# Edge counting in windows of 16 nodes instead of 32, and small operations shifted across five phase borders

## The reference

```python
xn = _layernorm(x)
x = x + gnn(xn, edge_index) + mix(xn[None])[0]
x = x + ffn(_layernorm(x)[None])[0]
```

```python
q, k, v = split(x @ qkv_w.T + qkv_b)                 # 8 heads of 96
phi_q = exp(einsum(q, rf) - q_norm); phi_k = exp(einsum(k, rf) - k_norm)
kv = einsum('bhnm,bhnd->bhmd', phi_k, v)
attn = einsum('bhnm,bhmd->bhnd', phi_q, kv) / maximum(denominator, 1e-6)
out = attn @ proj_w.T + proj_b
```

## Time and profile before

| | us |
|---|---|
| median of 3 runs | 2090.27 (2078.87 to 2092.76) |
| the profiled execution's own time | 2086.34 |
| its span | 2084.6 |
| PE busy in the span | 1991.5 (96%) |
| DVE busy in the span | 1168.3 (56%) |

### The profile page before, as it was taken

The page is one execution under the profiler, slowest core; times in us unless marked ns, Lnnn a source line. Parts: engine busy times, 40 slices in busy tenths (PEclk is TensorE's granted clock), DMA queues, the critical chain, the costliest instruction groups (busy, mean ns, idle before and its releaser), DMA issues. The chain is left out here.

```text
span 2084.6 us, 32353 instructions
## 1 busy us (share of the span) xinstructions
PE 1991.5 (96%) x9933; PEld 1469.9 (71%) x9934; DVE 1168.3 (56%) x2548; ACT 449.5 (22%) x822; POOL 176.6 (8%) x181
## 2 busy tenths in 40 slices
PE   4999899998989998999999999999997999999998
PEld 3666666666648887888888855556655777777776
DVE  6666436652565664888888652167764333333343
ACT  3222222222002321222222200004321222222222
POOL 0000000000000000000000000000001333222232
PEclk9999999998999999999999999999997999999999
DMA  7000220002645350743333244444225888899654
GB/s 257 22 17 20 93 107 17 20 17 74 217 120 171 121 155 32 221 146 102 122 101 112 82 153 156 151 134 142 90 74 196 271 249 241 252 284 289 180 136 83
DMA packets 81192, 282.79 MB, mean 136 GB/s; under 512 B 11689, under 2 KB 32225, under 8 KB 71490
## 3 DMA queue, kind: packets, MB, share of 16 engines
q1 hardware_dynamic: 59138, 211.02, 30.4%
q0 software_dynamic: 14848, 56.18, 11.1%
q10 hardware_dynamic: 7104, 14.26, 2.0%
HBM read 217.43 MB, written 63.99 MB: 135 GB/s over the span
## 5 line engine op out<-in xcount | busy, mean ns | idle before, releaser
L1379 PE MATMUL gat_Z<-h_head,first_rest 125*125 125x256 f32 (+1 forms) x1600 | 355.5, 381 | 3.3 <-DVEq L1283 3.3
L1379 PEld LDWEIGHTS gat_Z<-h_head,first_rest 125*125 125x125 f32 x1600 | 298.4, 189 | 49.2 <-issue 4.0
L762 PE MATMUL mix_G<-mix_w,xnT 128*125 128x384 f32 x720 | 243.0, 488 | 0.0
L762 PEld LDWEIGHTS mix_G<-mix_w,xnT 128*125 128x125 f32 x720 | 133.3, 189 | 85.1 <-issue 2.7
L2400 DVE TENSOR_SCALAR ex_idS<-ex_ids 128x1 int32 x52 | 8.0, 153 | 204.5 <-DMA out_rows<-ex_y,ex_idS 204.5
L2487 PE MATMUL ex_PH<-ex_xT,w_and_experts 128*128 128x128 f32 x936 | 111.1, 278 | 1.7 <-issue 0.2
L2487 PE MATMUL ex_PH<-ex_xT,ex_w 128*128 128x128 f32 x936 | 111.0, 278 | 0.8
L2487 PEld LDWEIGHTS ex_PH<-ex_xT,w_and_experts 128*128 128x128 f32 x936 | 106.5, 192 | 2.7 <-issue 2.7
L2497 PE MATMUL ex_PY<-w_and_experts,ex_hT 128*128 128x384 f32 x312 | 107.5, 495 | 0.3 <-ACT ex_hT L2434 0.3
L2497 PE MATMUL ex_PY<-ex_w,ex_hT 128*128 128x384 f32 x312 | 107.4, 494 | 0.3 <-ACT ex_hT L2434 0.3
L2487 PEld LDWEIGHTS ex_PH<-ex_xT,ex_w 128*128 128x128 f32 x936 | 106.5, 192 | 1.5 <-issue 1.3
(11 more groups left out here) (399 smaller groups left out, 3120.8 us busy)
## 6 DMA issues: line engine op xcount, KB each, us to landing
w_and_experts<-in_L_ffn_W SPq DMA_DIRECT2D x32, 1152.0 KB, 8.2
ex_w<-in_L_ffn_W SPq DMA_DIRECT2D x32, 1152.0 KB, 7.9
first_wide<-c_dram SPq DMA_DIRECT2D x40, 546.9 KB
h1T_dram<-gat_oT ACTq DMA_DIRECT2D x40, 250.0 KB, 2.0
mix_w<-in_L_mix_qkv_w SPq DMA_DIRECT2D x6, 1152.0 KB, 12.6
ct_dram<-mix_count_out SPq DMA_DIRECT2D x40, 157.0 KB, 2.1
mix_w_slice<-in_L_gnn_W SPq DMA_DIRECT2D x6, 1024.0 KB, 10.8
proj_w2s<-in_L_gnn_W SPq DMA_DIRECT2D x4, 1536.0 KB, 9.5
```

Of the source, the lines that this page charges most:

```text
L762: last = pe.matmul(G[c][:], xnT[:, k, t * P:(t + 1) * P], w[:, k, c, :], start=(k == 0), stop=(k == KD - 1))
L1379: last = pe.matmul(Z[b][j][:], wt[b][:, s, :], h[hd][0:P, s, j * HC:(j + 1) * HC + j], start=(s == 0), stop=(s == NT - 1))
```

## The change

**Counting.** A window has 16 destinations and eight parts of the sources (16 x 8 = 128 keys again) with 157 places each; there are 80 windows, four to a tile, steps of three rows and a ring of eight steps. S, CB and the stored rows are 157 wide. PE's order in a tile becomes: turn(0), GEMM q, A, turn(1), GEMM k, B, features 0, GEMM v, features 1, C, the first half of `keys_values`, its second half, D. DVE's: norms, A, B, evacuation of v, C, D, columns. ACT makes the squares for tile t+1 behind the count copy of window C of tile t. The part of a source is computed by an integer multiplication and a shift. The matmuls that open KV stand behind the three GEMMs of tile 0.

```diff
-RB = 5
+RB = 3
-WIN = 32
-NW = 40
-SPLIT = 4
-SLO = 314
+WIN = 16
+NW = 80
+SPLIT = 8
+SLO = 157
...
-    RING = 4
+    RING = 8
...
                         window(PER * t)
+                        window(PER * t + 1)
                         dve.wait_ge(v_done, t + 1)
-                        if t >= 1:
-                            dve.wait_ge(kv_step, t)
+                        if t == 0:
+                            dve.wait_ge(kv_opened, 2)
+                        else:
+                            dve.wait_ge(kv_step, 2 * t)
...
-                        window(PER * t + 1)
+                        window(PER * t + 2)
+                        window(PER * t + 3)
...
                     act.activation(kT[:], TQ[:], ACT.Copy).then_inc(kT_done, 1)
...
+                    keep_counts(PER * t + 1)
+                    for j in range(2):
+                        if (t, j) == (NT - 1, 1):
+                            keep_counts(PER * t + 2)
+                        act.wait_ge(phi, 2 * t + j + 1)
+                        if t >= 1:
+                            act.wait_ge(kv_step, 2 * (t - 1) + j + 1)
+                        act.activation(phik[:, 2 * j:2 * j + 2, :], PH[:], ACT.Exp).then_inc(exped, 1)
+                    if t + 1 < NT:
+                        keep_counts(PER * t + 2)
+                    if t + 1 < NT:
+                        squares(t + 1)
+                    keep_counts(PER * t + 3)
...
-                pe.wait_ge(consts, 2)
-                for j in range(2):
-                    pe.matmul(KV[j][:].rearrange("p h m a -> p (h m a)"), zero[:],
-                              vs[:].rearrange("p h a -> p (h a)"), start=True, stop=False, skip_group_check=True)
...
                     gemm(2, 0, v_done, v_evac)
+                    pe.wait_ge(consts, 2)
+                    for j in range(2):
+                        pe.matmul(KV[j][:].rearrange("p h m a -> p (h m a)"), zero[:],
+                                  vs[:].rearrange("p h a -> p (h a)"), start=True, stop=False, skip_group_check=True
+                                  ).then_inc(kv_opened, 1)
+                    pe.wait_ge(steps_ready, 1)
...
                         if more:
                             gemm(1, t + 1, k_done, k_evac)
+                        window(PER * t + 1, *span(pe, at + 1))
                         features(t, 0)
-                        window(PER * t + 1, *span(pe, half * PER * NT + PER * t + 1))
-                        features(t, 1)
                         if more:
                             gemm(2, t + 1, v_done, v_evac)
-                        keys_values(t, not more)
+                        if more:
+                            features(t, 1)
+                            window(PER * t + 2, *span(pe, at + 2))
+                        else:
+                            window(PER * t + 2, *span(pe, at + 2))
+                            features(t, 1)
+                            window(PER * t + 3, *span(pe, at + 3))
+                        keys_values(t, 0, not more)
+                        keys_values(t, 1, not more)
+                        if more:
+                            window(PER * t + 3, *span(pe, at + 3))
```

```diff
             copy(8)
-            dve.wait_ge(span_max, 1)
-            step(dve.tensor_scalar(allb[:, 0, :], allb[:, 0, :], -1.0, 1000.0, ALU.mult, ALU.add))
...
             copy(9)
...
+                if half == 0:
+                    dve.wait_ge(span_max, 1)
+                    window_steps(step, dve, allb, spi, spans)
+                dve.sem_inc(steps_ready, 1)
...
-            for b in range(XR):
-                sp.wait_ge(stores[b], 32 * len(range(b, NT, XR)))
...
-                if t >= 2:
-                    for k in range(2 * (t - 2), 2 * (t - 1)):
+                if 1 <= t <= KF // 2:
+                    for k in range(2 * (t - 1), 2 * t):
                         attention_columns(k)
...
-            cx.clear()
...
             sp.wait_ge(al_stored, 16)
+            for b in range(XR):
+                sp.wait_ge(x1_stored[b], 32 * len(range(b, NT, XR)))
...
-                    logits(1)
-                    scores(1)
+                    raw_logits(1)
                 tile_of(n, c22, p5_done, 1, 1, Y5)
+                if n == PAIRS - 1:
+                    slopes()
...
-                if n == PAIRS - 1:
-                    weights(1)
...
+                    if first and t == 0:
+                        weights(0, 1)
                     normalise(hd, t)
...
-            for b in range(2):
-                act.wait_ge(stored[b], H1 * HT16)
...
                 for i in range(2):
+                    sp.wait_ge(h1_stored[i], 16 * ((H1 - 1) * HT + n + 1))
                     sp.dma_start(pair[n % 2][:, i, :], h1T_dram[2 * n + i, :, :]).then_inc(in_loaded[n % 2], 16)
...
             c22_of(1)
+            c12_of(0)
             dve.wait_ge(row_loaded, 16)
             dve.wait_ge(mask_loaded, 32 * NT)
-            largest(0)
-            c12_of(0)
```

More of the change, by code:

```diff
@@ L106, in sem, with release @@
         return self.sems[-1]
+    def release(self, sems):
+        self.nc.clear_and_free_semaphores(sems)
+        self.sems = [s for s in self.sems if s not in sems]
     def clear(self):
@@ L157, in norm_phase @@
     REST = EDGES - FULL * PE_ROWS
-    DIV_SHIFT = 10
-    DIV = (1 << DIV_SHIFT) // RB + 1
+    PART_SHIFT = 17
+    PART = (1 << PART_SHIFT) // SLO + 1
+    assert all(n * PART >> PART_SHIFT == n // SLO for n in range(N)) and N * PART < 1 << 24
     assert FULL < EGP and EGP * EG == EROWS
-    assert all(n * DIV >> DIV_SHIFT == n // RB for n in range(EROWS + RB))
     with ExitStack() as st:
@@ L230, in _ @@
             step(dve.tensor_copy(sf[:], si[:]))
-            step(dve.tensor_scalar(hi[:], sf[:], float(SLO), None, ALU.is_ge))
-            for part in range(2, SPLIT):
-                step(dve.scalar_tensor_tensor(hi[:], sf[:], float(part * SLO), hi[:], ALU.is_ge, ALU.add))
+            step(dve.tensor_scalar(si[:], sf[:], float(PART), None, ALU.mult))
+            step(dve.tensor_scalar(si[:], si[:], PART_SHIFT, None, ALU.logical_shift_right))
+            step(dve.tensor_copy(hi[:], si[:]))
             step(dve.scalar_tensor_tensor(slo[:], hi[:], -float(SLO), sf[:], ALU.mult, ALU.add))
@@ L446, in proj_phase @@
     a2_loaded, wa2_step = cx.sem("proj_a2_loaded"), cx.sem("proj_wa2_step")
-    stores = [cx.sem(f"proj_stores{b}") for b in range(XR)]
     KC = 4
     w2_loaded = [cx.sem(f"proj_w2_loaded{c}") for c in range(KF // KC)]
+    cx.release(done_with)
     with ExitStack() as st:
@@ L729, in keep_counts, with squares @@
                     act.activation(cout[i % 2][:], S[:], ACT.Copy).then_inc(s_evac, 1)
-                for t in range(NT):
+                def squares(t):
                     for c, (evac, squared, ready) in enumerate(((q_evac, qsq, q_ready), (k_evac, ksq, k_ready))):
@@ L736, in _ @@
                         act.activation(sq[:, c, :, :], qs[:, c, :, 0:MD], ACT.Square).then_inc(squared, 1)
+                squares(0)
+                for t in range(NT):
                     act.wait_ge(q_turned, t + 1)
@@ L828, in _ @@
                             gemm(0, t + 1, q_done, q_evac)
-                        window(PER * t, *span(pe, half * PER * NT + PER * t))
+                        at = half * PER * NT + PER * t
+                        window(PER * t, *span(pe, at))
                         turn(1, t)
@@ L1049, in _ @@
                     dve.wait_ge(gat.rows_loaded[0], 32)
-                    logits(0)
+                    raw_logits(0)
+                    slopes()
                 if n == PAIRS - 1:
@@ L1113, in _ @@
                 if n == PAIRS - 1:
-                    for t in range(2):
-                        act.wait_ge(gat.e_ready, t + 1)
-                        act.activation(gat.e[t], gat.e[t], ACT.Exp).then_inc(gat.exp_done, 1)
+                    act.wait_ge(gat.e_ready, 1)
+                    act.activation(gat.e[0], gat.e[0], ACT.Exp).then_inc(gat.exp_done, 1)
         @block.tensor
@@ L1229, in gat1_phase @@
     u, e, wt, cnt = gat.u, gat.e, gat.wt, gat.cnt
-    stored = [cx.sem(f"gat1_stored{b}") for b in range(2)]
     HC = C1 // 2
@@ L1283, in _ @@
             dve.sem_inc(mn_ready, 2)
+            dve.tensor_tensor(e[1], u, rows[0][0:P, 1:2, P:2 * P].to_broadcast([P, NT, P]), ALU.subtract
+                              ).then_inc(e_ready, 1)
             dve.wait_ge(b_loaded, 16)
@@ L1345, in exp_scores @@
                 act.activation(e[t % 2], e[t % 2], ACT.Exp).then_inc(exp_done, 1)
+            exp_scores(0, 1)
             def body(hd, hb, first, last):
@@ L2604, in build @@
                                    attn, ins["L0_gnn_W1"], ins["L0_gnn_att_src1"], ins["L0_gnn_att_dst1"], wa, keyT,
-                                   sloT, spans, counting, ct_dram, load_half(1) if half == 0 else load_proj)
```

(7 more changed lines are left out.)

84 lines of the change are left out of this document (45 added, 39 removed).

## The result

The changed kernel takes 2109.44 us (median of 4 runs, 2105.68 to 2112.1) beside 2087.11 (4 runs) for the kernel before; the ratio is 1.0098 with a 95% interval of 1.0075 to 1.0121. It is slower by 20.5 us by the ratio, 22.3 by the medians, where the prediction had 2089, about 3 us slower, and "the same" as its likeliest outcome. The time lies inside the range, near its upper end.

What follows compares the result with a forecast made beforehand. PE, busy 1991.5 of 2084.6 us, was taken as the bound. Borders -15.45, window D +14.4 and last tiles +4 gave +2.95 on 2086.3: 2089 (own range 2074 to 2100), overall range 2058 to 2114.

Steps and rivals of the forecast that it cites:

- the clock: Rival in the mix tiles: D's sparse matmuls halve PE's clock, 2 us in each of 18 tiles: 2125, chance 0.13.
- window D: In each mix tile, behind `keys_values`: 1.8 us of register work exposed, tile 19.65, +0.80 each, +14.4 in all.
- the last tiles: Last tile of each half: four windows without a GEMM, paced by register work; +4 for both, between +1.5 and +8.
- The borders: Five phase borders, from normalisation to the project phase: work or waits leave PE's path, -15.45 us together.
- the start: Half 0's border: eleven operations leave the end of normalisation, KV opening moves later; -3.0 us (-2 to -5).
- The opening of half 1: Head of half 1: the KV opening moves later, hiding part of its 2.7 us wait; -1.2 us (0 to -2.7).
- Hidden: First rival, mix tiles: register work stays hidden, D costs its columns only; 18.2 us a tile, 2060, chance 0.22.
- DVE becomes the bound: Third rival, mix tiles: DVE sets the pace at its upper end, 20.3 us a tile; 2101, chance 0.12.
- No fewer columns: Fourth rival, counting: a window needs a third step, nine matmuls, more registers; chance 0.03 shared with a border turning round.

Runs made afterwards that it cites:

- the kernel with the borders alone: Changed kernel with the old counting (32-node windows, two a tile, five rows a step), five borders and later KV opening kept: 2073.34, ratio 0.9919.
- the fastest kernel: Changed kernel with windows C and D under cover, one CB instruction a step, ACT's squares before the second exponential, one PE register a window: 2062.91, ratio 0.9873.
- the cover alone: Changed kernel with window C in the middle of v's GEMM, D between features 1 and `keys_values`, ACT's copy of C moved: 2086.97, ratio 0.9991.
- a faster DVE: Changed kernel with DVE making the three CB rows of a step in one instruction instead of three, PE's order untouched: 2107.12 (one run).
- faster DVE windows: Changed kernel with windows C and D under cover and one CB instruction a step on DVE: 2083.97, ratio 0.9973.

## Why the prediction was wrong

The forecast was +2.95 us, the ratio gives +20.5. Of the 17.5 between them the clock is 10, window D 5 and the last tiles 2. That the time still lies inside the range is luck: the range left out most of the clock case, which came true at less than a third of its price (10 of 36 us).

**The borders: right.** -15.45 was forecast; the kernel with the borders alone has -16.3 by the medians. Single terms are off by 0.6 to 1.5 us each way; the start alone differs by more than that between profiles (half 0 begins at 50.0 to 54.2 us in the eight kernels that have the borders). The opening of half 1 gave half of its -1.2: from the numerator's last group (268.84 before, 284.26 after) to the first turn it takes 25.55 instead of 26.20, -0.65. The table has +0.2 there, since the numerator's first group, behind a last tile at the half clock, takes 0.9 longer. Before, the four opening matmuls waited for POOL, 2.7 us; but they also ran at the half clock that PE has after the pause there (granted 0.50 from 281 to 283 us). Now the first GEMM stands first, waits 2.0 for the block, and pays the half clock itself (0.50 from 296 to 298): its 36 matmuls take 13.54 us, 12.03 before. (First two rows: the kernel before; then the changed kernel.)

```profile
280.43 2.95 PE L796 MATMUL mix_KV<-mix_vs,mix_zero 125*128 125x388 f32 x4 [2.71 <-POOL mix_vs L643]
283.17 12.03 PE L762 MATMUL mix_G<-mix_w,xnT 128*125 128x384 f32 x36
```

```profile
295.12 13.54 PE L791 MATMUL mix_G<-mix_w,xnT 128*125 128x384 f32 x36 [2.00 <-PEq L390]
308.50 1.47 PE L851 MATMUL mix_KV<-mix_vs,mix_zero 125*128 125x388 f32 x4
```

**Window D: the mechanism was right, the size small.** "D is not [covered]", +0.80 a tile; it is +1.09, 19.6 us instead of 14.4. The start of its register work was met to a tenth: `keys_values` starts at 66.47 in one tile, the second exponential ends at 66.63, and the sequencer's load follows at 66.7 (instructions of L632 on PE's sequencer, 66 to 71 us).

```profile
L632 PEldq TENSOR_LOAD <-spans x2: 297/303/309, 66.7 to 70.7; - x2
```

From there to the next turn it takes 3.9 us, not the 3.6 that six of ten matmuls' time and one head gave: the change from the first step to the second costs as much for three rows as for five. The moves of C and D test this: with both under cover 22 us go (2086.97) and no window of these tiles stands without cover, with both uncovered the time grows by 88 us, nearly all of it in the 18 tiles (456.9 us instead of 369.3).

**The clock: a rival that came true in part.** This is the step that failed: the sum priced the clock behind window D at nothing. The prediction gave it 0.13, with 2 us in each of 18 tiles or nothing, and kept it out of the forecast because of one row: after a wait of 2.1 us in the project phase the clock stayed at 1.00. The chip did neither: the clock falls behind window D in some tiles, six of 18 in the changed kernel's profile at about 1.7 us each, 10 us in all. The prediction's own sign for this case, a granted clock under 1 in the mix tiles, is there. One row at 1.00 behind one pause was taken as what happens behind every thin stretch. The kernel before had nearer rows that showed the other outcome: in both its last tiles the clock fell while windows ran without cover (one stretch of each; columns as in group 9).

```profile
232.00:234.00 2.00, 1.45 (x5) 0.52 (x5) 1.97 (x7) 0.44 (x1) 0.00 (x0) 0.62 0.00 0
474.00:477.00 3.00, 3.00 (x10) 1.66 (x9) 0.00 (x0) 0.43 (x1) 0.00 (x0) 0.64 0.11 39
```

An average over "sometimes" belonged into the sum.

**The last tiles: +6.0 against +4**, within the bounds given: at half clock, 0.50 from 240 to 255 us, the `keys_values` of half 0 take 3.70, 2.02 before. (The sum's 4 x 3.6 + 1.8 is 16.2, not 16.3.) Not all of the +6.0 is the smaller windows: with the old counting and the borders alone the last tile of half 0 took 19.2 us too, 2.5 more than in the profile before, by the clock.

**The other rivals.** *Hidden*: fallen, the waits for issue at every window D say so. Its number, 2060, is nearly reached by the fastest kernel, 2062.91, but that took the cover and three further edits; the cover alone gives 2086.97. *DVE becomes the bound*: not in the changed kernel (17.0 us of waits for ACT are left in nine tiles, and a faster DVE changed nothing), but it is the next bound, as the cover kernel's 19.35 shows: faster DVE windows took 0.3 us off each tile there and nothing off the 19.9 of the changed kernel. *No fewer columns*: fallen, two steps in each window seen.

Adding up with the measured terms: -16.3 for the borders, +19.6, +10 and +6 in the mix make +19.3, beside +20.5 by the ratio. If the 2.5 of the last tile are already in the -16.3, it is +16.8.

What stays open: which window D lowers the clock. With the same work of PE in each tile it was each third tile in one profile and two of 18 in another.

## What to carry to other kernels

Smaller pieces of work with addresses in registers cost a fixed time of the sequencer each, here 3.7 to 3.9 us a window against 0.45 of matmuls; before cutting work finer, count for each piece what dense work stands between its register loads and its turn, and place the pieces so that this time is always larger. Here the place of two windows on PE was worth 22 us, more than the 14.2 that the smaller windows save in matmuls; and it took three more edits, on DVE, on ACT and in the register loads, before the counting clearly gained something beyond the borders. And a stretch of few matmuls is paid twice where the clock falls behind it, in some repetitions only, so its price is better averaged over many rows than read from one.

## What the runs showed that was not expected

- Removing a bound uncovered the next three times: PE's window D (20.5 a tile), DVE's register work (about 19.1), ACT's squares in front of DVE's norms (18.8), and only then the sum of the matmuls (18.06).
- The register loads on PE start only when the waits of what stands before them on that engine are met: 66.7, just behind the exponential that ends at 66.63, and 230.7 in rows 3, where the features group in front of it starts at 230.68. In none of the ten profiles does a window's first load start with more than 17 pairs of weight load and matmul still ahead of it, 34 instructions. The Trainium skill, "TensorE: Matmul & The Clock Gate" (opening table), gives TensorE a queue of 64 entries. The traces stay at about half of that.
